# Folding the softmax factor into the masked-maximum pass of a two-layer attention and feed-forward kernel

## The chip, the cores and the metric

The kernel runs on one core of a Trainium2 chip. The metric is the device time of one execution in microseconds (us); lower is better. A profiled execution also has a span, from its first to its last instruction.

## What the kernel must compute

Two pre-norm transformer layers on x of shape (4, 256, 256), all float32. Each layer adds an attention block and then a feed-forward block to x. Only the attentions bear on the change:

```
layer 0:  q = rms_norm(x Wq) ; k = rms_norm(x Wk)          16 query heads, 8 key/value heads, head width 128
          q, k = rope(q), rope(k)
          logits = (q * 0.0884) k^T ;  masked to j <= i and i - j < 128
          probs  = softmax(logits) ;   out = (probs v) Wo
layer 1:  scores = (x Wq)(x Wk)^T                          16 heads, width 128
          masked to j <= i, then / sqrt(128)
          probs  = softmax(...) ;      out = (probs v) Wo
```

The softmax is computed in the stable form: exp of (scaled logit minus the row's largest scaled logit), divided by the row's sum. In layer 0 the query's RMS normalisation is not applied to q: the query's row factor `rms_r` is a factor per row of the logits, so it can be applied after the product q k^T. The feed-forward of layer 0 is a gated one with a 2-of-4 sparsification, that of layer 1 has a Walsh-Hadamard transform that is folded into its second weight matrix.

## The kernel before, in words

Tokens are 1024 rows in 8 tiles of 128. Each attention works on 64 units: 8 head pairs times 4 sequences times 2 heads. A unit is one head of one sequence of 256 rows. Its scores are two blocks, rows 0 to 127 against 128 keys (columns 0 to 127 of a bank) and rows 128 to 255 against 256 keys (columns 128 to 383).

The attention is a software pipeline written out by hand in slots c = -5 to 70. In slot c each engine does a fixed list of pieces, each for another unit or token tile, and semaphores join the engines (`need`, line 62). Slots 11 to 58 are a hardware loop of 3 turns of 16 slots; the slots before and after are written out. The order inside a slot is the program order of each engine:

- TensorE (`pe_slot`, L254): scores of unit c (L250, L251); the projection of piece c+5 (L273 in layer 0, L279 and L308 in layer 1); the output product of piece c-6 (L296); the transposes of unit c-2 (L317); the product with v of unit c-3 (L328, L330); in layer 0 the transposes of tile c+3 (L339).
- ScalarE, ACT (`act_slot`, L345): copies of what TensorE left for units c-3 and c-4 (L352, L360) and of pieces c+4 and c+2 (L368, L370, L377, L384, L392), and last the two exps of unit c (L402). The next slot's copies stand behind these exps in ScalarE's queue.
- VectorE, DVE (`dve_slot`, L460): reciprocal and normalisation of unit c-1 (L411, L414), residual add of piece c-7 (L422), low part of the encoding of unit c-4 (L431), the masked maxima of unit c (L447) and the negated, scaled maxima (L453 in layer 0, L457 in layer 1); in layer 0 then the RMS sums and the rotation of tile c+4 (L482, L486, L490, L493). In the last slots, from 60 on, the maxima come first.
- GpSimd, POOL (`pool_slot`, L504): in layer 0 the power -1/2 that gives `rms_r` and the rest of the rotation (L513, L515, L519); in both layers the splits of the next pair's weights into high and low parts (L500, L502). In slots 1 to 6 of layer 1 it also makes one butterfly of the Hadamard transform per slot (L961).

The masked maximum is one VectorE instruction per block: (scores + mask) * scale, with scale 1, written to `scores`, and the running maximum of it read out to `rowmax`. A small instruction then makes `negmax` = -rowmax * factor, and the exp computes exp(factor * scores + negmax) with the row sum as a second output. The factor is the row factor `rms_r` in layer 0 (an operand of one value per partition) and the constant 1/sqrt(128) in layer 1.

Of the kernel before, what the change touches and what calls it, by code (L numbers as in the profile page):

```python
# [39 lines left out]
RMS_EPS = 1e-6  # L40
ATTN_SCALE = 0.08838834764831845
ROPE_BASE = 10000.0
LOW = -3.0e38
MASKED = -1.0e30
WA = (1024, 1536)
WA_FFN = 2048
# [32 lines left out]
def build(nc, x_in, wa, wax, wb, wdown0, w2t, consts, scales, out):  # L79
    with ExitStack() as ctx:  # L80
        def sb(name, shape, dt=F32):
            return ctx.enter_context(nc.sbuf_tensor(name, shape, dt))

        def sem(name):
# [18 lines left out]
        scores = sb("scores", [P, 2, 384])  # L103
        probs = sb("probs", [P, 4, 384])
        probs_t = sb("probs_t", [P, 2, 384])
        rowmax = sb("rowmax", [P, 2, 2])
        negmax = sb("negmax", [P, 2, 2])
        rowsum = sb("rowsum", [P, 4, 2])
        rinv = sb("rinv", [P, 4, 2])
# [39 lines left out]
        s_scl, s_w2 = sem("scales_loaded"), sem("w2_loaded")  # L149
        s_zero, s_half, s_tab, s_scq = (sem(n) for n in ("zero_set", "half_set", "tables_made", "qscale_made"))  # L150
        ln = {n: sem("ln_" + n) for n in ("stats", "mv", "ve", "r", "xn", "turned", "hi", "lo")}
        names = ("scores", "max", "nb", "exp", "rinv", "pnorm", "pt", "ptev", "pv", "ehi", "elo", "op", "opadd",
                 "proj", "vproj", "qkev", "vev", "sq", "ss", "ms", "rp", "rot", "radd", "roped", "tq", "tqev",
                 "a0hi", "a0", "ahi", "a", "bhi", "b")
        at = [{n: sem(f"L{L}_{n}") for n in names} for L in range(2)]
# [189 lines left out]
        def act_slot(act, L, it, c):  # L345
            s = at[L]

            m = c - 3
            if live(it, m):
                need(act, s["pt"], it, m + 1)  # L350
                need(act, s["pv"], it, m - 1)
                nc.scalar.copy(probs_t[:, m % 2, :], bank[PT_BANK][:, 0:384]).then_inc(s["ptev"], 1)  # L352

            m = c - 4
            if live(it, m):
                u = m % 8
                b, hh = u // 2, u % 2
                need(act, s["pv"], it, m + 1)
                need(act, s["op"], it, m - hh - 6)
                nc.scalar.copy(enc[0][:, hh, b * D:(b + 1) * D], bank[O_BANK][:, 0:D]).then_inc(s["ehi"], 1)  # L360
            m = c + 4
            if live(it, m):
                t = m % 8
                need(act, s["proj"], it, m + 1)
                if L == 0:

                    need(act, s["ss"], it, m)
                    nc.scalar.activation(squares[:, :], bank[PJ_BANK + m % 2][:, 0:384], ACT.Square).then_inc(s["sq"], 1)  # L368
                    need(act, s["pv"], it, m - t % 2 - 14)
                    nc.scalar.copy(v[:, m // 8 % 2, t, 0:DH], bank[PJ_BANK + m % 2][:, 384:512]).then_inc(s["vev"], 1)  # L370
                else:
                    half, w = t // 4, t % 4
                    need(act, s["scores"], it, m - t + 4 * half - 4)
                    if it is None and m in (0, 2):
                        act.wait_ge(ff[0]["lo"], 10 + m)
                        act.wait_ge(ff[0]["lo23"], 2 + m)
                    nc.scalar.copy(qk[:, w, half * 512:(half + 1) * 512], bank[PJ_BANK + m % 2][:, :]).then_inc(s["qkev"], 1)  # L377

                    need(act, s["vproj"], it, m + 1)
                    need(act, s["pv"], it, m - t % 2 - 14)  # L380
                    if it is None and m == 0:

                        act.wait_ge(ff[0]["cmp"], 24)
                    nc.scalar.copy(v[:, m // 8 % 2, t, :], bank[TQ_BANK][:, 0:D]).then_inc(s["vev"], 1)  # L384
            if L == 0:

                m = c + 2
                if live(it, m):
                    t = m % 8
                    need(act, s["tq"], it, m + 1)  # L390
                    need(act, s["scores"], it, m - t % 2 - 6)
                    nc.scalar.copy(qk[:, 0:3, t * P:(t + 1) * P],  # L392
                                   bank[TQ_BANK][:, 0:384].rearrange("p (a t) -> p a t", a=3)).then_inc(s["tqev"], 1)

            if live(it, c):
                u = c % 8
                b, hh = u // 2, u % 2
                need(act, s["nb"], it, c + 1)
                need(act, s["pt"], it, c - 3)
                for r, (c0, c1) in enumerate(((0, 128), (128, 384))):  # L400
                    scale = rms_r[:, 2 * b + r, hh:hh + 1] if L == 0 else float(DH) ** -0.5
                    nc.scalar.activation(probs[:, c % 4, c0:c1], scores[:, c % 2, c0:c1], ACT.Exp,  # L402
                                         bias=negmax[:, c % 2, r:r + 1], scale=scale,
                                         accum_out=rowsum[:, c % 4, r:r + 1]).then_inc(s["exp"], 1)

        def dve_normalise(dve, L, it, c):
# [27 lines left out]
        def dve_scores_wait(dve, L, it, c):  # L434

            s = at[L]
            if live(it, c):
                need(dve, s["scores"], it, c + 1)
                need(dve, s["exp"], it, 2 * c - 2, 2)

        def dve_maxima(dve, L, it, c):

            s = at[L]
            if live(it, c):
                b, hh = c % 8 // 2, c % 2
                for r, (c0, c1) in enumerate(((0, 128), (128, 384))):
                    nc.vector.tensor_tensor_reduce(out=scores[:, c % 2, c0:c1], in0=bank[S_BANK + c % 2][:, c0:c1],  # L447
                                                   in1=mask[L][:, c0:c1], scale=1.0, scalar=LOW, op0=ALU.add, op1=ALU.max,
                                                   accum_out=rowmax[:, c % 2, r:r + 1]).then_inc(s["max"], 1)
                need(dve, s["max"], it, 2 * c + 2, 2)  # L450
                if L == 0:
                    need(dve, s["rp"], it, c - hh + 2)
                    nc.vector.scalar_tensor_tensor(out=negmax[:, c % 2, :], in0=rowmax[:, c % 2, :], scalar=-1.0,  # L453
                                                   in1=rms_r[:, 2 * b:2 * b + 2, hh], op0=ALU.mult,
                                                   op1=ALU.mult).then_inc(s["nb"], 1)
                else:
                    nc.vector.tensor_scalar(negmax[:, c % 2, :], rowmax[:, c % 2, :], -float(DH) ** -0.5, None,  # L457
                                            ALU.mult).then_inc(s["nb"], 1)

        def dve_slot(dve, L, it, c):  # L460
            s = at[L]
# [42 lines left out]
        def pool_slot(pool, L, it, c):  # L504
            s = at[L]
            if L == 0:
                m = c + 3
                if live(it, m):
                    t = m % 8

                    need(pool, s["ms"], it, m + 1)
                    need(pool, s["exp"], it, 2 * (m - t % 2) - 12, 2)
                    nc.gpsimd.tensor_tensor(rms_r[:, t, :], meansq[:, m % 2, :], neg_half[:, 0:3], ALU.pow).then_inc(s["rp"], 1)  # L513
                    need(pool, s["rot"], it, m + 1)
                    nc.gpsimd.tensor_tensor(rot_a[:, m % 2, :], rot_a[:, m % 2, :], rot_b[:, m % 2, :],  # L515
# [590 lines left out]
        def _(dve):  # L1106
# [6 lines left out]
            nc.vector.tensor_tensor(a_w[0][1][:, 0:WA[0]], raw_a[:, 0, 0:WA[0]], a_w[0][0][:, 0:WA[0]].bitcast(F32),  # L1113
                                    ALU.subtract).then_inc(at[0]["a0"], 1)
            dve.wait_ge(s_scl, 16)
            nc.vector.tensor_scalar(scl[:, 0::2, :], scl[:, 0::2, :], ATTN_SCALE, None, ALU.mult).then_inc(s_scq, 1)
            for t in range(4):
                ln_dve_lo(dve, 0, t, 4 + t)

# [90 lines left out]
def shape_constants(np):  # L1210
# [7 lines left out]
    low = np.float32(MASKED)  # L1218
    tri = np.where(past, np.float32(0), low)
    win = np.where(window, np.float32(0), low)  # L1220
    mask0 = np.concatenate([tri, win, tri], 1)
    mask1 = np.concatenate([tri, np.zeros((P, P)), tri], 1)
    frac = np.arange(0, DH, 2, dtype=np.float32) / np.float32(DH)
    timescale = (np.float32(ROPE_BASE) ** frac).astype(np.float32)
# [52 lines left out]
```

## Time and profile before

| what | value |
|---|---|
| time, median of 3 runs | 768.96 us (768.14 to 769.33) |
| span of the profiled execution | 763.1 us |
| median less span (what lies around the span) | 5.9 us |
| PE busy | 712.4 us, 93% of the span |
| DVE busy | 549.9 us, 72% |
| ACT busy | 415.8 us, 54% |
| POOL busy | 404.2 us, 53% |
| mean granted TensorE clock | 0.987 of full |

No time of its own is given for the profiled execution beside its span, so times are compared through the difference to the median. Stages by time from the span's start: start up to about 34 us, attention of layer 0 to about 291 us, feed-forward of layer 0 to about 396 us, attention of layer 1 to about 690 us, feed-forward of layer 1 to the end. The busy time of an engine is that of its instructions; an instruction that is held after it has been handed to its engine counts as busy for as long as it is held.

### The profile page before, as it was taken

The page shows a single profiled execution, that of the slowest core. Times are in us where ns is not written, and L with a number is a line of the kernel's source. Part 1 is how long each engine was busy: PE and PEld are TensorE (multiplying, and loading weights), DVE is VectorE, ACT ScalarE, POOL GpSimd, SP SyncE. Part 2 cuts the span into 40 slices and gives each one's busy share as a digit, 9 for nine tenths or more (in the row PEclk, how much of TensorE's full clock was granted, in tenths as well). Part 3 has the DMA queues.
Part 4 walks back from the last instruction along what each step waited for, and adds up shares of the span by engine and source line. Part 5 has one row for each costly group of instructions (what it writes and reads, how often), then busy time and mean ns, then how long its engine had stood idle before and what let it go on. Part 6 is the DMA issues. An engine that isn't in the chain of part 4 may idle for free.

```text
span 763.1 us, 15137 instructions
## 1 busy us (share of the span) xinstructions
PE 712.4 (93%) x4360; PEld 633.9 (83%) x4360; DVE 549.9 (72%) x1861; ACT 415.8 (54%) x1213; POOL 404.2 (53%) x545
## 2 busy tenths in 40 slices
PE   4899999999999969986888999999999999989998
PEld 3589999899899967775776899999999999877887
DVE  7898987988898897979867655555545555576533
ACT  3577777677677754430344556555555655644221
POOL 4898888788787856526387523233241514416000
PEclk9999999999999999988999999999999999999999
DMA  6011010101110110300101010101010100000000
GB/s 220 2 43 32 12 43 2 42 0 41 58 67 0 55 56 1 110 1 1 42 1 56 1 56 1 56 1 55 0 55 0 60 36 14 1 14 1 1 28 28
DMA packets 9015, 24.75 MB, mean 32 GB/s; under 512 B 896, under 2 KB 3072, under 8 KB 8832
## 3 DMA queue, kind: packets, MB, share of 16 engines
q1 hardware_dynamic: 8240, 22.55, 8.6%
q10 hardware_dynamic: 720, 1.57, 0.6%
q8 instruction: 22, 0.36, 0.2%
q14 instruction: 33, 0.27, 0.1%
HBM read 23.07 MB, written 1.05 MB: 32 GB/s over the span
## 4 chain that ended last, share of the span: by engine, by line
PE 80%; DVE 12%; issue 4%; ACT 1%; POOL 1%; DMA 1%; DVEq 0%; SPq 0%; ACTq 0%; POOLq 0%
PE bank L296 11%; PE bank L597 10%; PE bank L279 10%; PE bank L273 10%; PE bank L328 7%; PE bank L251 6%; PE bank L308 5%; PE bank L317 5%; PE bank L630 5%; PE bank L330 3%; PE bank L250 3%; PE bank L339 3%; DVE work L814 2%; DVE probs L414 1%; PE bank L655 1%
## 5 line engine op out<-in xcount | busy, mean ns | idle before, releaser
L500 POOL TENSOR_TENSOR a_hi<-raw_a,zero 128x384 fp32r<-128x384 f32 (+2 forms) x75 | 60.4, 805 | 116.7 <-PE bank L308 115.0
L431 DVE TENSOR_TENSOR enc_lo<-bank,enc_hi 128x256 fp32r<-128x256 f32 x128 | 54.2, 423 | 74.2 <-PE bank L251 66.0
L402 ACT ACTIVATE probs<-scores,negmax,rms_r 128x128 f32<-128x128 f32 (+1 forms) x128 | 69.1, 540 | 61.1 <-DVE negmax L453 61.1
L414 DVE TENSOR_SCALAR probs<-probs,rinv 128x128 f32<-128x128 f32 (+1 forms) x256 | 90.9, 397 | 4.5
L352 ACT COPY probs_t<-bank 128x384 f32<-128x384 f32 x128 | 60.6, 474 | 57.5 <-PE bank L317 56.6
L402 ACT ACTIVATE probs<-scores,negmax 128x128 f32<-128x128 f32 (+1 forms) x128 | 57.2, 448 | 58.0 <-DVE negmax L457 58.0
L447 DVE CUSTOM_DVE_ANT_0 scores<-bank,cst 128x128 f32<-128x128 f32 (+1 forms) x256 | 80.0, 350 | 3.5 <-PE bank L251 3.5
L296 PE MATMUL bank<-b_hi,enc_hi 128*128 128x256 f32 x256 | 73.7, 288 | 9.3 <-DVE x L422 9.1
L328 PE MATMUL bank<-probs_t,v 128*128 128x256 f32 x256 | 77.0, 383 | 2.9 <-DVE enc_lo L431 2.8
L251 PE MATMUL bank<-qk 128*128 128x256 f32 x256 | 76.9, 382 | 0.0
L502 POOL TENSOR_TENSOR a_lo<-raw_a,a_hi 128x384 fp32r<-128x384 f32 (+2 forms) x75 | 72.8, 970 | 5.9
L513 POOL TENSOR_TENSOR rms_r<-meansq,neg_half 128x3 f32<-128x3 f32 x64 | 57.8, 904 | 33.4 <-DVE meansq L490 33.1
L296 PE MATMUL bank<-b_lo,enc_hi 128*128 128x256 f32 x256 | 72.1, 282 | 0.0
L296 PE MATMUL bank<-b_hi,enc_lo 128*128 128x256 f32 x256 | 72.0, 281 | 0.0
L411 DVE RECIPROCAL rinv<-rowsum 128x2 f32<-128x2 f32 x128 | 20.3, 159 | 66.4 <-ACT probs L402 62.2
L515 POOL TENSOR_TENSOR rot_a<-rot_a,rot_b 128x384 f32<-128x384 f32 x64 | 66.6, 1041 | 0.0
L273 PE MATMUL bank<-a_hi,xT_hi 128*128 128x512 f32 x128 | 62.1, 485 | 4.5 <-DVE rot_b L493 3.5
L279 PE MATMUL bank<-xT_hi,a_hi 128*128 128x512 f32 x128 | 62.1, 485 | 0.9 <-DVE xT_lo L226 0.9
L317 PE MATMUL bank<-cst,probs 128*128 128x128 f32 x384 | 62.7, 272 | 0.2 <-ACT probs_t L352 0.2
L296 PEld LDWEIGHTS bank<-b_hi,enc_hi 128*128 128x128 f32 x256 | 48.3, 189 | 16.8 <-issue 10.4
L360 ACT CAST enc_hi<-bank 128x256 fp32r<-128x256 f32 x128 | 47.6, 372 | 20.7 <-PE bank L330 20.1
L500 POOL TENSOR_TENSOR b_hi<-raw_b,zero 128x128 fp32r<-128x128 f32 (+1 forms) x68 | 30.3, 446 | 47.3 <-PE bank L296 47.3
(106 smaller groups left out, 2216.2 us busy)
## 6 DMA issues: line engine op xcount, KB each, us to landing
raw_a<-in_wa SPq DMA_DIRECT2D x10, 768.0 KB, 4.4
raw_a<-in_wa SPq DMA_DIRECT2D x9, 512.0 KB, 4.4
raw_b<-in_wb SPq DMA_DIRECT2D x16, 256.0 KB, 2.7
x<-in_x SPq DMA_DIRECT2D x4, 256.0 KB, 5.9
w_a<-in_w2t SPq DMA_DIRECT2D x1, 1024.0 KB, 4.8
raw_a<-in_wax SPq DMA_DIRECT2D x2, 512.0 KB, 3.2
raw_b<-in_wdown SPq DMA_DIRECT2D x2, 512.0 KB, 3.8
raw_a<-in_wa ACTq DMA_DIRECT2D x1, 512.0 KB, 4.6
```

Source lines behind the costliest of these rows:

```text
L251: pe.matmul(ps[:, 128:384], qk[:, q, t0 + 128:t0 + 256], qk[:, k, t0:t0 + 256], start=True, stop=True).then_inc(s["scores"], 1)
L273: mm = pe.matmul(ps[:, :], xT[l][:, g, t * P:(t + 1) * P], a_w[slot][r][:, g * 512:(g + 1) * 512], start=i == 0, stop=i == 5)
L279: mm = pe.matmul(ps[:, :], a_w[slot][l][:, g * 768 + w * P:g * 768 + (w + 1) * P], xT[r][:, g, half * 512:(half + 1) * 512], start=i == 0, ...
L296: mm = pe.matmul(output_bank(m)[:, 0:D], enc[l][:, h, t * P:(t + 1) * P], b_w[slot][r][:, h * D:(h + 1) * D], start=i == 0, stop=i == 5)
L317: mm = pe.transpose(bank[PT_BANK][:, j * P:(j + 1) * P], probs[:, m % 4, j * P:(j + 1) * P], ident)
L328: pe.matmul(bank[O_BANK][:, 0:256], v[:, m // 8 % 2, 2 * b, vc:vc + DH], probs_t[:, m % 2, 0:256], start=True, stop=False, skip_group_chec ...
L402: nc.scalar.activation(probs[:, c % 4, c0:c1], scores[:, c % 2, c0:c1], ACT.Exp, bias=negmax[:, c % 2, r:r + 1], scale=scale, accum_out=ro ...
L414: nc.vector.tensor_scalar(probs[:, m % 4, c0:c1], probs[:, m % 4, c0:c1], rinv[:, m % 4, r:r + 1], None, ALU.mult).then_inc(s["pnorm"], 1)
L447: nc.vector.tensor_tensor_reduce(out=scores[:, c % 2, c0:c1], in0=bank[S_BANK + c % 2][:, c0:c1], in1=mask[L][:, c0:c1], scale=1.0, scalar ...
L500: nc.gpsimd.tensor_tensor(hi, src, zero[:, 0:1].broadcast_to(list(src.shape)), ALU.add).then_inc(s_hi, 1)
L502: nc.gpsimd.tensor_tensor(lo, src, hi.bitcast(F32), ALU.subtract).then_inc(s_lo, 1)
L597: mm = pe.matmul(ps[:, :], a_w[t][l][:, c0:c0 + P], xT[rr][:, g, th * 512:(th + 1) * 512], start=q == 0, stop=q == 5)
```

## The change

The factor moves from the exp into the masked-maximum pass. `scale` of the pass becomes the factor, with the sign turned, so what is written to `scores` is minus the scaled logit; the reduction is a minimum instead of a maximum; its result is minus the largest scaled logit, which is `negmax` itself. The instruction that made `negmax` and the tile `rowmax` go away, with the semaphore `nb`. The exp takes `scale=-1.0` in both layers. In layer 1 the factor is the constant -1/sqrt(128). In layer 0 it is the row factor `rms_r`, one value per partition, and the sign comes from the query's scale table and from a mask of the other sign.

The waits move as well: ScalarE waits for each block's own minimum ahead of that block's exp, where it waited once for `nb`; VectorE's wait for `rms_r` stands with the wait for the scores, ahead of L431; GpSimd waits for the minima and not for the exps before it writes `rms_r` again.

```diff
             if live(it, c):
-                u = c % 8
-                b, hh = u // 2, u % 2
-                need(act, s["nb"], it, c + 1)
                 need(act, s["pt"], it, c - 3)
                 for r, (c0, c1) in enumerate(((0, 128), (128, 384))):
-                    scale = rms_r[:, 2 * b + r, hh:hh + 1] if L == 0 else float(DH) ** -0.5
+                    need(act, s["max"], it, 2 * c + 1 + r, 2)
                     nc.scalar.activation(probs[:, c % 4, c0:c1], scores[:, c % 2, c0:c1], ACT.Exp,
-                                         bias=negmax[:, c % 2, r:r + 1], scale=scale,
+                                         bias=negmax[:, c % 2, r:r + 1], scale=-1.0,
                                          accum_out=rowsum[:, c % 4, r:r + 1]).then_inc(s["exp"], 1)
...
                 need(dve, s["scores"], it, c + 1)
                 need(dve, s["exp"], it, 2 * c - 2, 2)
+                if L == 0:
+                    need(dve, s["rp"], it, c - c % 2 + 2)
...
                 for r, (c0, c1) in enumerate(((0, 128), (128, 384))):
+                    scale = rms_r[:, 2 * b + r, hh:hh + 1] if L == 0 else -float(DH) ** -0.5
                     nc.vector.tensor_tensor_reduce(out=scores[:, c % 2, c0:c1], in0=bank[S_BANK + c % 2][:, c0:c1],
-                                                   in1=mask[L][:, c0:c1], scale=1.0, scalar=LOW, op0=ALU.add, op1=ALU.max,
-                                                   accum_out=rowmax[:, c % 2, r:r + 1]).then_inc(s["max"], 1)
-                need(dve, s["max"], it, 2 * c + 2, 2)
-                if L == 0:
-                    need(dve, s["rp"], it, c - hh + 2)
-                    nc.vector.scalar_tensor_tensor(out=negmax[:, c % 2, :], in0=rowmax[:, c % 2, :], scalar=-1.0,
-                                                   in1=rms_r[:, 2 * b:2 * b + 2, hh], op0=ALU.mult,
-                                                   op1=ALU.mult).then_inc(s["nb"], 1)
-                else:
-                    nc.vector.tensor_scalar(negmax[:, c % 2, :], rowmax[:, c % 2, :], -float(DH) ** -0.5, None,
-                                            ALU.mult).then_inc(s["nb"], 1)
+                                                   in1=mask[L][:, c0:c1], scale=scale, scalar=HIGH, op0=ALU.add, op1=ALU.min,
+                                                   accum_out=negmax[:, c % 2, r:r + 1]).then_inc(s["max"], 1)
...
-                    need(pool, s["exp"], it, 2 * (m - t % 2) - 12, 2)
+                    need(pool, s["max"], it, 2 * (m - t % 2) - 12, 2)
                     nc.gpsimd.tensor_tensor(rms_r[:, t, :], meansq[:, m % 2, :], neg_half[:, 0:3], ALU.pow).then_inc(s["rp"], 1)
...
-            nc.vector.tensor_scalar(scl[:, 0::2, :], scl[:, 0::2, :], ATTN_SCALE, None, ALU.mult).then_inc(s_scq, 1)
+            nc.vector.tensor_scalar(scl[:, 0::2, :], scl[:, 0::2, :], -ATTN_SCALE, None, ALU.mult).then_inc(s_scq, 1)
...
-    mask0 = np.concatenate([tri, win, tri], 1)
+    mask0 = -np.concatenate([tri, win, tri], 1)
```

## Rows read from the trace of the kernel before

**Rows 1.** The profile page: busy time of each engine, and the chain that ended last.

```profile
PE 712.4 (93%) x4360; PEld 633.9 (83%) x4360; DVE 549.9 (72%) x1861; ACT 415.8 (54%) x1213; POOL 404.2 (53%) x545
...
PE 80%; DVE 12%; issue 4%; ACT 1%; POOL 1%; DMA 1%; DVEq 0%; SPq 0%; ACTq 0%; POOLq 0%
```

**Rows 2.** Busy time by window: stretch, length, busy (instructions), clock, DMA share, GB/s.

```profile
50.00:127.90 77.90, 77.90 (x503) 71.26 (x502) 70.06 (x271) 56.71 (x176) 65.11 (x98) 1.00 0.07 22
...
262.00:291.00 29.00, 22.30 (x157) 19.64 (x156) 26.60 (x92) 15.67 (x48) 17.15 (x21) 1.00 0.12 37
...
400.00:426.00 26.00, 20.91 (x110) 16.94 (x108) 20.39 (x41) 10.87 (x36) 21.40 (x19) 0.93 0.11 41
426.00:670.00 244.00, 241.83 (x1578) 222.31 (x1579) 132.84 (x563) 142.88 (x443) 78.73 (x113) 1.00 0.08 26
670.00:694.00 24.00, 21.43 (x129) 17.14 (x128) 17.02 (x69) 10.92 (x33) 3.91 (x7) 1.00 0.05 12
```

**Rows 3.** Groups of instructions by form, whole span: busy us, mean ns, idle before.

```profile
L447 DVE CUSTOM_DVE_ANT_0 scores<-bank,cst 128x256 f32<-128x256 f32 x128 | 53.6, 419 | 0.0
...
L402 ACT ACTIVATE probs<-scores,negmax,rms_r 128x256 f32<-128x256 f32 x64 | 37.5, 586 | 0.0
...
L402 ACT ACTIVATE probs<-scores,negmax 128x256 f32<-128x256 f32 x64 | 31.6, 494 | 0.0
...
L457 DVE TENSOR_SCALAR negmax<-rowmax 128x2 f32<-128x2 f32 x64 | 18.1, 283 | 2.2
L453 DVE SCALAR_TENSOR_TENSOR negmax<-rowmax,rms_r 128x2 f32<-128x2 f32 x64 | 16.3, 255 | 2.2
```

**Rows 4.** VectorE groups by form in 670 to 691 us, GpSimd nearly idle.

```profile
L206 DVE TENSOR_SCALAR xn<-x,ln_mv,ln_r 128x256 f32<-128x256 f32 x4 | 1.6, 398 | 0.0
...
L414 DVE TENSOR_SCALAR probs<-probs,rinv 128x256 f32<-128x256 f32 x3 | 1.0, 348 | 0.0
```

**Rows 5.** TensorE's waits, 396 to 428 us: total us, times, longest.

```profile
PE bank L308 <- ACT v L384: 3.5, 4, 1.3
PE bank L328 <- DVE enc_lo L431: 1.7, 2, 0.8
```

**Rows 6.** Timeline of VectorE in layer 1's first slots: start, duration (us).

```profile
400.22 2.17 DVE L457 TENSOR_SCALAR negmax<-rowmax 128x2 f32<-128x2 f32 x1
...
406.52 0.17 DVE L457 TENSOR_SCALAR negmax<-rowmax 128x2 f32<-128x2 f32 x1
...
411.73 0.28 DVE L447 CUSTOM_DVE_ANT_0 scores<-bank,cst 128x128 f32<-128x128 f32 x1
...
415.32 2.88 DVE L414 TENSOR_SCALAR probs<-probs,rinv 128x128 f32<-128x128 f32 x2
...
419.11 2.34 DVE L457 TENSOR_SCALAR negmax<-rowmax 128x2 f32<-128x2 f32 x1
```

**Rows 7.** Timeline of GpSimd in the same slots.

```profile
399.98 2.38 POOL L961 TENSOR_TENSOR work<-w_a 128x1024 f32<-128x1024 f32 x1
...
411.62 2.42 POOL L961 TENSOR_TENSOR w_a<-work 128x1024 f32<-128x1024 f32 x1
...
419.08 2.35 POOL L961 TENSOR_TENSOR work<-w_a 128x1024 f32<-128x1024 f32 x1
```

**Rows 8.** Timeline of TensorE: the same matmuls in two slots.

```profile
412.79 0.60 PE L328 MATMUL bank<-probs_t,v 128*128 128x256 f32 x2
...
415.26 0.40 PE L279 MATMUL bank<-xT_hi,a_lo 128*128 128x512 f32 x1
...
418.67 0.87 PE L328 MATMUL bank<-probs_t,v 128*128 128x256 f32 x2 [0.83 <-DVE enc_lo L431]
...
422.85 0.40 PE L279 MATMUL bank<-xT_hi,a_lo 128*128 128x512 f32 x1
```

**Rows 9.** The end of layer 0's attention, 262 to 284 us: VectorE group, TensorE's wait.

```profile
L453 DVE SCALAR_TENSOR_TENSOR negmax<-rowmax,rms_r 128x2 f32<-128x2 f32 x5 | 2.8, 558 | 0.2
```

```profile
PE bank L296 <- DVE x L422: 5.0, 3, 3.0
```

More of the change, by code:

```diff
@@ L42 @@
 ROPE_BASE = 10000.0
-LOW = -3.0e38
+HIGH = 3.0e38
 MASKED = -1.0e30
@@ L105, in build @@
         probs_t = sb("probs_t", [P, 2, 384])
-        rowmax = sb("rowmax", [P, 2, 2])
         negmax = sb("negmax", [P, 2, 2])
@@ L151, in build @@
         ln = {n: sem("ln_" + n) for n in ("stats", "mv", "ve", "r", "xn", "turned", "hi", "lo")}
-        names = ("scores", "max", "nb", "exp", "rinv", "pnorm", "pt", "ptev", "pv", "ehi", "elo", "op", "opadd",
+        names = ("scores", "max", "exp", "rinv", "pnorm", "pt", "ptev", "pv", "ehi", "elo", "op", "opadd",
                  "proj", "vproj", "qkev", "vev", "sq", "ss", "ms", "rp", "rot", "radd", "roped", "tq", "tqev",
```

## The prediction, made before the changed kernel ran

> **What bounds the kernel now.** I read the page first, then the windows by stage, the waits of TensorE, and the timelines of the stretches in which TensorE stands still. The page says that TensorE is busy 93% of the span and makes up 80% of the chain that ended last, VectorE 12% [rows 1]. So a VectorE instruction less is worth nothing on average; the question is where TensorE waits for VectorE. The windows answer it [rows 2]. In the steady slots of layer 0 (50 to 127.9 us) TensorE is busy 77.90 of 77.90 us, in those of layer 1 (426 to 670 us) 241.83 of 244. TensorE stands still at the end of layer 0's attention (6.7 of 29.0 us), in the first slots of layer 1's attention (5.1 of 26.0 us, with the granted clock down to 0.93) and at that attention's end (2.6 of 24.0 us). Only these stretches can pay.
>
> The first slots of layer 1 carry my forecast. The small instruction L457 has 64 instances with a mean of 283 ns [rows 3], but it is not the same everywhere: 0.17 us at 406.52, and 2.17 us at 400.22 and 2.34 us at 419.11 [rows 6]. The GpSimd rows explain these two: the Hadamard butterflies L961 run from 399.98 to 402.36 and from 419.08 to 421.43, and L457 ends at 402.39 and 421.45, just behind them [rows 7]. It is held while GpSimd works. L414 is held too (2.88 us for two at 415.32), while L447 is not: at 411.73 it takes its usual 0.28 us in the midst of the butterfly that began at 411.62 [rows 6, 7]. Behind a held L457 stands the exp, behind the exp the next slot's copies of ScalarE, and TensorE waits for the copy L384 four times, 3.5 us, and for L431 twice, 1.7 us [rows 5].
>
> **The change part by part.** *Layer 1, first slots.* L457 goes, with 5 instances between 399 and 426 us. Undisturbed it is 0.17 us; the two that I show cost 2.0 and 2.2 us more. A third such case has the same pattern behind the butterfly of 411.62. What is late next is L414, which needs a gap between GpSimd instructions for each of its two halves. Before, a slot took three such gaps (L457, L414, L414) and an exp between them, so that slots locked to two butterflies each: the held L457 at 419.11 follows a held L414 at 415.32. After, one slot needs two gaps, and from the second of them to the next L414 lie L431, half of L447, two exps of one block each, and L411, roughly 1.9 us; so a slot locks to one butterfly, and these come on average 3.7 us apart (411.62 and 419.08 are two butterflies apart [rows 7]). TensorE's own slot there is about as long. Walking the queues of the four engines through slots 0 to 6 with these durations, the copies and the enc_lo are ready 1 to 5 us before TensorE gets to them, and all six waits close. That is 3.5 + 1.7 = 5.2 us [rows 5]. The exp of the first block may also start before the second block's minimum, 0.42 us earlier by L447's mean [rows 3]; that only adds to the margin.
>
> The waits also carry a lower clock. In one slot the matmuls from the first L328 to the last L279 take from 412.79 to 415.66, 2.87 us; in the next from 418.67 to 423.25, 4.58 us, though nothing among them waits [rows 8]. Just before, TensorE had waited, the last time for 0.83 us [rows 8]; part of the second run is at the lower of its two levels (1.2 against 2.4 GHz). With the waits gone I take the 1.7 us as gone too. Bounds: 5.2 + 1.7 = 6.9 us if all closes; 2.0 us if L414 takes over what L457 leaves. I take 6.9, since the hand-made walk leaves margin at each of the six.
>
> *Layer 0, last slots.* TensorE waits 5.0 us in three places for the residual add L422 [rows 9], which stands in VectorE's queue behind L447, L453, L411 and L414. Five L453 there take 558 ns in the mean, 2.8 us in all [rows 9]; with 0.17 us each for the work, as L457 takes when nothing holds it [rows 6], 1.9 us of it is holding. It does not all come back: L414 is next in the queue and meets the same GpSimd instructions. In my walk the first slot gives nothing (L414's second half ends behind the same GpSimd instruction), the second 0.3 us, the third about 1 us. Bounds: 0 (L414 takes all) to 2.8 us; I take 1.2, nearer to the walk.
>
> *Layer 0, the added operand.* The pass now reads one value per partition. No row before has that on a reduction with a PSUM input. Nearest: L206 with two such operands takes 398 ns at 128x256, L414 with one takes 348 [rows 4], so about 50 ns for one. Two passes make 0.10 us a slot, against L453's mean of 0.26 us that goes [rows 3]. Bounds per pass: 0, to 92 ns, which is what the row factor costs the exp (586 against 494 ns [rows 3]). In the steady slots all of it lies beside TensorE: 503 matmuls at 26 a slot are 19.3 slots of 4.03 us, in which VectorE idles 7.84 us, 0.41 us a slot [rows 2]. So even 2 x 92 ns with no saving at all costs nothing. The cover is gone at 0.41 us a slot.
>
> *The exps.* In layer 0 they lose 92 ns each and start earlier; in layer 1 their scale was a constant already. ScalarE is busy 56.7 of 77.9 us [rows 2], so this is hidden except in the last slots, where it is within the 1.2.
>
> *The moved waits.* VectorE's wait for `rms_r` now stands ahead of L431 and L447. In slot c it asks for tile c+1 at most, which GpSimd made two slots earlier, so it is met. GpSimd's wait for minima in place of exps is for a unit four slots back, met either way. No DMA moves. The sign changes in the tables cost nothing: same instructions.
>
> *The rest.* In the start, VectorE's queue is on the chain for a few slots, and so it is for one instruction's worth at each turn of the loop in layer 0: 0.3 us in all (0 to 0.8). At the end of layer 1's attention TensorE is idle 2.6 us, most of it behind the layer norm and the held L414; 0.2 us (0 to 1). In the steady slots of layer 1 nothing.
>
> **Sum.** 6.9 + 1.2 + 0.3 + 0.2 = 8.6 us. The span 763.1 becomes 754.5; the median lies 5.9 us above the span before, and so the time is 768.96 - 8.6 = 760.4 us. All of it is carried to the end, because what follows each stretch hangs on TensorE or on the work right behind it.
>
> **The rivals.** *A. The lock moves on.* L414 takes the holding that L457 leaves in layer 1: only the 2.0 us of the first L457, and half of layer 0's 1.2, come back. For it: L414 is held already, 2.88 us at 415.32. Against it: a slot needs one GpSimd gap less. 768.96 - 2.6 - 0.5 = 765.9 us.
>
> *B. The waits close but the clock does not stay up*, since TensorE has other short waits just before this stretch and merely loses the clock elsewhere: 1.7 us less, 762.1 us.
>
> *C. The new pass is held by GpSimd in layer 0.* Slower than before. With its row factor in SBUF the pass has two SBUF operands, as L453 has, and each of the two passes of a slot then waits for a gap. GpSimd is busy 65.1 of 77.9 us with 98 instructions, 0.66 us each [rows 2]; the first pass waits 0.84 x 0.66 / 2 = 0.3 us, the second for the whole next instruction, 0.66 us. With 0.10 for the operand that is 1.06 us, less 0.26 for L453: 0.8 us a slot against a cover of 0.41. Slots get 0.39 us longer in about 58 steady slots, 22.6 us: 768.96 + 22.6 - 6.9 = 784.7 us. It decides from 0.41 us a slot on. Against it: L453 itself, with two SBUF operands, is held only 0.1 us in the mean, and by the same mean the two passes would add 0.04 us net and stay covered.
>
> The Trainium skill (SBUF — State Buffer, Who interferes with whom) speaks against the change here: VectorE and GpSimd share one pair of ports, locked for a whole instruction, and a VectorE instruction contends for it in a 2-port mode or with two SBUF inputs, but not with at most one. It does not say whether a value per partition counts as an input. If it does, case C is the result and the time 784.7 us; if not, the forecast stands. The trace agrees with the rule for L447, one SBUF input and not held inside a butterfly [rows 6, 7]; no row before shows a pass with the added value.
>
> *D. No change*, because TensorE is busy 93% of the time and the waits in layer 1's first slots have another cause such as the first exp's table load: 768.9 us. Against it: waits of VectorE and ScalarE that end with the butterflies.
>
> **How the numbers follow.** The forecast has 0.66, A 0.11, B 0.12, C 0.05 (with other ways to be slower 0.07), D 0.04. A measurement of this kernel tells 0.2%, 1.5 us, from no change. Faster: 0.66 + 0.11 + 0.12 = 0.89; same 0.04; slower 0.07. The range reaches down to 757.0 us (layer 0's end at its 2.8 in place of 1.2, the start and layer 1's end at 1.8 in place of 0.5: 757.5, and a little for closer packing) and up to 765.0 us (half-way from B to A and beyond), which leaves out C, D and most of A, under 0.2.
>
> **What would show it.** Right: no instruction between L447's second half and L411 or L482; TensorE's waits for L384 and L431 in layer 1's first slots gone, and granted clock 1.00 in that window, its slots 3.7 us each; the longest L414 still 2 to 3 us; the pass in layer 0 at about 470 ns for 128x256 (419 + 50), in layer 1 still 419; exps of layer 0 at 494 ns; the steady slot of layer 0 still 4.03 us. Wrong: a pass in layer 0 with a mean over 0.7 us and a longer slot (C); TensorE still waiting for L384 behind an exp that is late because L414 was held (A); a lower clock somewhere else in attention 1 (B); slots 0 to 5 of layer 1 as long as before (D).

## The result, and the profile after

| | median | range | ratio to before, 95% interval |
|---|---|---|---|
| before | 768.55 us (4 runs) | 767.78 to 769.33 | |
| changed | 758.55 us (4 runs) | 754.81 to 759.08 | 0.9863 (0.9837 to 0.9889) |

The forecast was 760.4 us, range 757.0 to 765.0. The medians lie 10.0 us apart (8.5 to 12.5 by the interval of the ratio); I had said 8.6.

The page after gives the engines' busy times and the chain, which answer to [rows 1]. TensorE's share of the chain rises from 80 to 86%, VectorE's falls from 12 to 8%.

```profile
PE 713.8 (94%) x4360; PEld 637.9 (84%) x4360; DVE 519.8 (69%) x1733; ACT 409.6 (54%) x1213; POOL 404.5 (53%) x545
...
PE 86%; DVE 8%; issue 3%; POOL 1%; DMA 1%; ACT 1%; SPq 0%; DVEq 0%; ACTq 0%; POOLq 0%
```

Now the stretches of [rows 2] in the changed kernel (same columns: stretch, length, TensorE, its loads, VectorE, ScalarE, GpSimd, clock, DMA share, GB/s). The steady slots of layer 0 are TensorE's as before. In the first slots of layer 1 TensorE is busy 24.08 of 25.00 us at clock 1.00, where it was busy 20.91 of 26.00 us at 0.93. But the end of layer 0's attention shows a clock of 0.86 and that of layer 1 one of 0.94, which the first profile had at 1.00.

```profile
50.00:127.90 77.90, 77.90 (x502) 71.16 (x501) 67.61 (x252) 53.55 (x174) 64.98 (x98) 1.00 0.07 22
...
260.00:285.00 25.00, 21.23 (x132) 19.27 (x131) 19.77 (x69) 12.78 (x42) 15.91 (x18) 0.86 0.14 50
...
395.00:420.00 25.00, 24.08 (x143) 21.33 (x144) 16.59 (x52) 17.08 (x50) 22.70 (x23) 1.00 0.12 43
...
660.00:690.00 30.00, 26.57 (x149) 21.69 (x150) 20.22 (x80) 11.98 (x35) 6.60 (x11) 0.94 0.04 10
```

The groups by form answer to [rows 3]. The pass with a value per partition takes 479 ns for 128x256, with a constant 419; the exps are of one kind. L453 and L457 are gone. (Line numbers shift: the pass L447 is L446 now, the exp L402 is L398, the normalisation L414 is L410, the residual add L422 is L418, the product L296 is L295.)

```profile
L398 ACT ACTIVATE probs<-scores,negmax 128x256 f32<-128x256 f32 x128 | 64.1, 501 | 0.0
...
L446 DVE CUSTOM_DVE_ANT_0 scores<-bank,cst,rms_r 128x256 f32<-128x256 f32 x64 | 30.7, 479 | 0.0
L446 DVE CUSTOM_DVE_ANT_0 scores<-bank,cst 128x256 f32<-128x256 f32 x64 | 26.8, 419 | 0.0
```

The shortest, median and longest of all 128 passes with a value per partition, of both widths (ns, then first and last start):

```profile
L446 DVE CUSTOM_DVE_ANT_0 scores<-bank,cst,rms_r x128: 332/410/483, 27.5 to 277.7; 128x128 f32<-128x128 f32 x64, 128x256 f32<-128x256 f32 x64
```

TensorE's waits from 392 to 425 us, the answer to [rows 5]: those for the copy L384 and for L431 are gone, and what is left, the layer norm ahead of the first slot, was there before (0.9 and 0.2 us as well).

```profile
PE bank L278 <- DVE xT_lo L225: 0.9, 1, 0.9
PE bank L212 <- DVE xn L205: 0.2, 1, 0.2
```

VectorE and GpSimd in three of these slots (two timelines; start, duration): L410, the normalisation, is still held, 1.8 to 2.3 us for its two halves, but nothing else is, and each of these slots has one butterfly (L951, which was L961). VectorE's passes start at 408.22, 412.29, 415.95 and 419.73, so 3.7 to 4.1 us apart.

```profile
408.22 0.28 DVE L446 CUSTOM_DVE_ANT_0 scores<-bank,cst 128x128 f32<-128x128 f32 x1
...
409.77 2.26 DVE L410 TENSOR_SCALAR probs<-probs,rinv 128x128 f32<-128x128 f32 x2
...
412.29 0.28 DVE L446 CUSTOM_DVE_ANT_0 scores<-bank,cst 128x128 f32<-128x128 f32 x1
...
413.89 1.80 DVE L410 TENSOR_SCALAR probs<-probs,rinv 128x128 f32<-128x128 f32 x2
...
415.95 0.28 DVE L446 CUSTOM_DVE_ANT_0 scores<-bank,cst 128x128 f32<-128x128 f32 x1
...
419.73 0.27 DVE L446 CUSTOM_DVE_ANT_0 scores<-bank,cst 128x128 f32<-128x128 f32 x1
```

```profile
409.15 2.37 POOL L951 TENSOR_TENSOR w_a<-work 128x1024 f32<-128x1024 f32 x1
...
412.38 2.38 POOL L951 TENSOR_TENSOR w_a<-work 128x1024 f32<-128x1024 f32 x1
```

**Where the time went, by stage.** The stages are cut at the first matmul of the feed-forward of layer 0, at the first and at the last projection of layer 1's attention. "Clock" is TensorE's busy time times (1 - granted clock), summed over windows of 2 us, for the four stages in order. It is an estimate of the most that the lower clock can have cost: where TensorE would otherwise have waited, slower matmuls cost nothing.

| profile | span | layer 0 attention | feed-forward 0 | layer 1 attention | rest | of it clock |
|---|---|---|---|---|---|---|
| before, first | 763.1 | 292.0 | 85.6 | 281.8 | 103.7 | 0 + 7.9 + 1.5 + 0 |
| before, second | 767.4 | 294.4 | 84.7 | 284.7 | 103.6 | 4.4 + 5.3 + 3.1 + 0 |
| changed, first | 757.1 | 291.1 | 86.5 | 274.3 | 105.2 | 3.0 + 7.6 + 0 + 1.7 |
| changed, second | 751.1 | 289.6 | 83.4 | 274.5 | 103.6 | 0 + 5.3 + 0 + 0 |

Layer 1's attention is 7.3 to 10.4 us shorter. Layer 0's is 0.9 to 4.8 us shorter, and that depends on which executions one compares. The rest differs by its clock share. The feed-forward of layer 0 does not: without that share it has 77.7, 79.4, 78.9 and 78.1 us. Part of this is only where the cut before it falls, so layer 0 is better read as both its stages together without their clock shares: 369.7 and 369.4 us before, 367.0 and 367.7 after, 1.7 to 2.7 us shorter. The spans also say how far one pair of profiles can mislead: the two first ones lie 6.0 us apart, the two second ones 16.3.

### The profile page after: what moved, and what is told of

Its sections match the earlier page's. It is cut to its first block, busy times and chain, and to the rows that moved or that the text cites. A ratio compares the mean times of both kernels' runs of the same rounds, so it can differ in the third digit from the quotient of the medians.

```text
span 757.1 us, 15084 instructions
## 1 busy us (share of the span) xinstructions
PE 713.8 (94%) x4360; PEld 637.9 (84%) x4360; DVE 519.8 (69%) x1733; ACT 409.6 (54%) x1213; POOL 404.5 (53%) x545
## 4 chain that ended last, share of the span: by engine, by line
PE 86%; DVE 8%; issue 3%; POOL 1%; DMA 1%; ACT 1%; SPq 0%; DVEq 0%; ACTq 0%; POOLq 0%
PE bank L295 12%; PE bank L278 11%; PE bank L272 10%; PE bank L587 10%; PE bank L327 7%; PE bank L250 7%; PE bank L307 6%; PE bank L316 5%; PE bank L620 5%; PE bank L329 4%; PE bank L249 4%; PE bank L338 3%; DVE work L804 2%; PE bank L645 1%; DMA x<-in_x 1%
## 5 line engine op out<-in xcount | busy, mean ns | idle before, releaser
L398 ACT ACTIVATE probs<-scores,negmax 128x128 f32<-128x128 f32 (+1 forms) x256 | 115.5, 452 | 42.5 <-DVE negmax L446 41.9
L427 DVE TENSOR_TENSOR enc_lo<-bank,enc_hi 128x256 fp32r<-128x256 f32 x128 | 54.2, 424 | 121.7 <-PE bank L250 111.0
L410 DVE TENSOR_SCALAR probs<-probs,rinv 128x128 f32<-128x128 f32 (+1 forms) x256 | 86.7, 380 | 4.5
L295 PE MATMUL bank<-b_hi,enc_hi 128*128 128x256 f32 x256 | 75.4, 294 | 5.9 <-DVE x L418 5.9
L295 PE MATMUL bank<-b_hi,enc_lo 128*128 128x256 f32 x256 | 72.7, 284 | 0.0
L295 PE MATMUL bank<-b_lo,enc_hi 128*128 128x256 f32 x256 | 72.7, 284 | 0.0
L295 PEld LDWEIGHTS bank<-b_hi,enc_hi 128*128 128x128 f32 x256 | 49.0, 191 | 11.6 <-issue 7.3
L329 PEld LDWEIGHTS bank<-probs_t,v 128*128 128x128 f32 x256 | 49.3, 193 | 6.9
L688 ACT ACTIVATE gate<-bank 128x512 f32<-128x512 f32 x32 | 19.0, 598 | 64.6 <-PE bank L587 56.2
L418 DVE TENSOR_TENSOR x<-bank,x 128x256 f32<-128x256 f32 x128 | 53.2, 416 | 0.0
```

The costliest lines, as they stand in the source:

```text
L295: mm = pe.matmul(output_bank(m)[:, 0:D], enc[l][:, h, t * P:(t + 1) * P], b_w[slot][r][:, h * D:(h + 1) * D], start=i == 0, stop=i == 5)
L329: pe.matmul(bank[O_BANK][:, 128:256], v[:, m // 8 % 2, 2 * b + 1, vc:vc + DH], probs_t[:, m % 2, 256:384], start=False, stop=True, skip_gr ...
L410: nc.vector.tensor_scalar(probs[:, m % 4, c0:c1], probs[:, m % 4, c0:c1], rinv[:, m % 4, r:r + 1], None, ALU.mult).then_inc(s["pnorm"], 1)
```

## The experiments

All kernels are compared with the kernel before on the same chip. Ratios have their 95% interval. A gain in us below is worked out from the ratio unless two medians are named.

**Layer 1 alone** (`l1_only`) and **layer 0 alone** (`l0_only`). The edit is the change itself with `if L == 1` or `if L == 0` around it, the other layer as before (the kernel is abridged here):

```diff
+                if L == 1:
+                    ... tensor_tensor_reduce(..., scale=-float(DH) ** -0.5, op1=ALU.min, accum_out=negmax[...])
+                else:
                     ... as before, with rowmax and L453
```

> The change in layer 1 alone; layer 0 as before. Theory (the small instruction L457 was held by GpSimd's butterflies in layer 1's first slots): nearly all of the gain of the whole change, 9 to 10 us of the 10.0, so a ratio of 0.988 to 0.991; TensorE's waits for L384 and L431 in the first slots gone. Rival (the gain is a bit less VectorE work in every place, in both layers alike): about half of it, ratio 0.994.

> The change in layer 0 alone; layer 1 as before. Theory: 0 to 2 us faster (0.9975 to 1.000), the steady slot still 4.03 us, all of it at the end of layer 0's attention; the waits in layer 1's first slots (5.2 us) still there. Rival (both layers alike): 5 us faster, ratio 0.994. If the operand of one value per partition were held by GpSimd, the pass would take over 700 ns for 128x256 here.

Measured: layer 1 alone 759.04 us, ratio 0.9895 (0.9873 to 0.9917), so 8 us; layer 0 alone 764.32 us, 0.996 (0.994 to 0.9979), so 3 us. Multiplied, the two ratios make 0.9855. The theory expected 9 to 10 us (a ratio of 0.988 to 0.991) and 0 to 2 us; the rival 5 and 5. Most is layer 1's, but layer 0 is worth more than either the theory's share or my forecast of 1.5. TensorE's waits in layer 1's first slots with layer 0 changed alone are those of before, to the tenth:

```profile
PE bank L309 <- ACT v L385: 3.5, 4, 1.3
PE bank L329 <- DVE enc_lo L437: 1.7, 2, 0.8
```

and with layer 1 changed alone only the layer norm's are left. With layer 0 changed alone the pass with a value per partition takes 479 ns as well.

**The small instruction in its place, but not held** (`l1_unheld`). The kernel before, one instruction exchanged for a form that was never held in the profile (L411). The kernel leaves out the factor: the exp of layer 1 subtracts another number than the scaled maximum, in the same time.

```diff
-                    nc.vector.tensor_scalar(negmax[:, c % 2, :], rowmax[:, c % 2, :], -float(DH) ** -0.5, None,
-                                            ALU.mult).then_inc(s["nb"], 1)
+                    nc.vector.reciprocal(negmax[:, c % 2, :], rowmax[:, c % 2, :]).then_inc(s["nb"], 1)
```

> The kernel before, but layer 1's L457 is a reciprocal of the same two columns: the same place, the same waits, about the same 0.16 us, in a form that is never held (L411). The factor's value is not computed, so layer 1's softmax is not the reference's. Theory (the lock): nearly the whole gain of the change in layer 1 comes back although no instruction is removed: 6 to 9 us faster, ratio 0.988 to 0.992. Rival (an instruction less in the chain and the exp's earlier start make the gain): within 1.5 us of the kernel before.

Measured: 760.71 us, ratio 0.9912 (0.989 to 0.9933), 6.8 us faster than before with not one instruction less. In its trace L457 is a reciprocal of 166 ns mean (283 before) and 167 ns at most, also where it starts in the midst of a butterfly, as at 413.36 us beside the one from 412.79 to 415.18; and TensorE waits for neither copy nor enc_lo in the first slots. This is the run that settles the cause: it is the holding. What is left for the rival, an instruction less in the chain, is the difference of this kernel to layer 1 alone, 1.3 us by the ratios, and their intervals overlap, so it is not told from nothing.

```profile
L457 DVE RECIPROCAL negmax<-rowmax 128x2 f32<-128x2 f32 x64 | 10.6, 166 | 2.2
```

```profile
413.36 0.17 DVE L457 RECIPROCAL negmax<-rowmax 128x2 f32<-128x2 f32 x1
```

**Short butterflies** (`small_bf_before`, `small_bf_after`). The other side of the holding: GpSimd's L961 is cut to 8 columns, in the kernel before and in the changed one. Both leave out nearly all of the Hadamard transform. The cut takes away what holds L457 and what holds the normalisation alike.

```diff
-                nc.gpsimd.tensor_tensor(b[:, :, n % 2, :], a[:, :, 0, :], a[:, :, 1, :],
+                nc.gpsimd.tensor_tensor(b[:, 0:1, n % 2, 0:8], a[:, 0:1, 0, 0:8], a[:, 0:1, 1, 0:8],
```

> The kernel before with the six Hadamard butterflies on GpSimd cut to 8 columns (the transform of the weights is left out but for these, so layer 1's feed-forward is not the reference's). Theory (the long GpSimd instructions hold L457): L457's mean falls from 283 ns to under 200, TensorE's waits in layer 1's first slots close, 6 to 9 us faster than the kernel before with the small instruction still in place, ratio 0.988 to 0.992. Rival (the instruction's own place in the chain costs): under 2 us faster.

> The changed kernel with the same small butterflies. Theory: without the long instructions the change is worth only what it is worth in layer 0 and a little in layer 1's last slots: 2 to 4 us faster than the kernel before with small butterflies, and within 1.5 us of the changed kernel, ratio to the kernel before 0.985 to 0.988. Rival: the full 10 us again, so 8 us or more between the two kernels with small butterflies.

Measured: before with short butterflies 759.97 us, ratio 0.9893 (0.9868 to 0.9917); the same with the change 756.89 us, 0.9847 (0.9813 to 0.9881). So the short butterflies alone give 8 us with L457 left as it is, and the change on top of them 3 us by the medians, as much as layer 0 alone gives. L457's mean fell only to 203 ns, not under 200: the weight splits hold it as well, for shorter (0.36 us at 402.92, behind the split from 402.86 to 403.26). The group:

```profile
L457 DVE TENSOR_SCALAR negmax<-rowmax 128x2 f32<-128x2 f32 x64 | 13.0, 203 | 2.2
```

**One wait for both minima** (`both_minima`). The changed kernel, with the exp's earlier start taken away:

```diff
-                    need(act, s["max"], it, 2 * c + 1 + r, 2)
+                    need(act, s["max"], it, 2 * c + 2, 2)
```

> The changed kernel, but both exps of a unit wait for both minima, as before, in place of each for its own. Theory: the earlier start only adds margin; time within 0.2% of the changed kernel (758.6 us), at most 1 us later. Rival (the exp's earlier start is a main part of the gain): 3 us or more slower than the changed kernel, 762 us or later.

Measured: 756.84 us, ratio 0.9854 (0.9825 to 0.9882), not to be told from the changed kernel. The earlier start is worth nothing that these runs can show.

**The two kernels again** (`after_again`, `before_again`).

> The changed kernel once more, unedited, as the yardstick of this set. Both theories: ratio 0.9863 as before, within its interval 0.984 to 0.989; executions spread over some 4 us with the mean granted clock (0.982 to 0.99).

> The kernel before, unedited, for a second profile. Its executions range from 764.8 to 771.5 us with the granted clock, and the profile I predicted from has the span of the fastest of them. Theory: the stretches without a lower clock are as long as in the first profile within 0.5 us, and whatever the span has above 763 us is clock, in stages where TensorE waits. Rival: another wait that the first profile did not have.

Measured: the changed kernel 757.92 us (753.02 to 760.58, more than the 4 us of spread I expected), ratio 0.9874 (0.9843 to 0.9904). The second profile of before, with a time of 769.03 us and a span of 767.4, is in the table above. Its clock fell at the end of layer 0's attention and longer than before in layer 1's first slots, after 424 us. But the rival is partly right too: the stretches without a lower clock are not as long within 0.5 us. TensorE waits 5.2 us for the copy L384 (3.5 in the first profile), in longer single waits (2.3 against 1.3 us). VectorE's side is the same in both: its passes L447 for slots 0 to 6 lie between 399.54 and 429.71 us in the first profile, 30.2 us, and between 401.06 and 431.25 in the second, 30.2 us too. What differs is TensorE's clock. In the first profile it was low around 421 us (0.50 from 420 to 422), TensorE came later to its next wait, and that wait was 0.67 us; in the second the clock was still full there and the same wait was 2.34 us. So the low clock of the first profile cost nothing on top of the waits. In the second it fell behind the last held slot and did cost: TensorE's slot from 429.03 us took 6.47 us, where the first profile has 4.46. At the end of layer 0 TensorE waits 3.9 us for L422 against 5.0; there too the clock is the lower one in the second profile (0.50 in the windows from 270 to 278 us).

The same wait in the first profile and in the second, then the second profile's sums and windows:

```profile
423.92 0.39 PE L308 MATMUL bank<-a_hi,xT_hi 128*128 128x256 f32 x1 [0.67 <-ACT v L384]
```

```profile
425.48 0.39 PE L308 MATMUL bank<-a_hi,xT_hi 128*128 128x256 f32 x1 [2.34 <-ACT v L384]
```

```profile
PE bank L308 <- ACT v L384: 5.2, 4, 2.3
PE bank L328 <- DVE enc_lo L431: 1.6, 2, 0.8
```

```profile
424.00:428.00 4.00, 1.79 (x10) 1.48 (x11) 3.90 (x8) 1.43 (x5) 3.92 (x3) 0.82 0.00 0
428.00:432.00 4.00, 4.00 (x12) 3.28 (x12) 2.84 (x12) 2.38 (x8) 3.56 (x7) 0.50 0.01 2
```

**The turns of layer 0's loop** (`padded`, `padded_one`). In the kernel before VectorE stood still for 2.07 and 2.14 us at the two turns of layer 0's loop, with no releaser ("issue"), and TensorE then waited 0.6 us for L422. In every kernel with layer 0 changed both are gone; in all in which layer 0 is as before they are there. Its loop body had shrunk from 271 to 254 instructions, counted without those that only wait for a semaphore, and the traffic of one instruction queue over the whole execution from 33 packets to 22. This is the stall in the first profile of before, and the queue before and after:

```profile
130.51 0.55 DVE L493 TENSOR_TENSOR rot_b<-bank,sin_t 128x384 f32<-128x384 f32 x1
133.13 0.17 DVE L411 RECIPROCAL rinv<-rowsum 128x2 f32<-128x2 f32 x1 [2.07 <-issue]
```

```profile
q14 instruction: 33, 0.27, 0.1%
```

```profile
q14 instruction: 22, 0.18, 0.1%
```

The edits to the changed kernel, 17 short instructions in the loop body or one long one:

```diff
+                    for i in range((1 + (c == LOOP_FROM)) if it is not None else 0):
+                        nc.vector.memset(scratch[:, 2 * (c - LOOP_FROM) + i:2 * (c - LOOP_FROM) + i + 1], 0.0)
```
```diff
+                    if it is not None and c == LOOP_FROM + LOOP_STEP - 1:
+                        nc.vector.memset(scratch[:, :], 0.0)
```

> The changed kernel with 17 one-column memsets of an unused tile added to VectorE's loop body of layer 0, one per slot and two in the first, so that the body has as many instructions as before (271; the changed kernel has 254). In the kernel before VectorE stood still for 2.1 us at each of the two turns of this loop with no releaser, and TensorE then waited 0.6 us for the residual add; in the changed kernel neither is there. Theory (the length of the body decides whether a turn stalls): the two stalls of 2.1 us are back, TensorE waits 0.2 to 0.6 us at each turn, layer 0's attention 0.5 to 1.2 us longer. Rival (the shorter VectorE work gives slack enough to hide the turn): no stall, as the memsets take about 0.07 us a slot of 0.5 us of slack.

> Control to the padded kernel: one memset of 512 columns in the last slot of layer 0's VectorE loop body, so more work right before the turn but 255 instructions. Theory of the length: no stall at the turns. Rival (slack): a stall or a wait of TensorE at the turns as in the padded kernel.

Measured: no stall in either, 758.68 us, ratio 0.9888 (0.9849 to 0.9926), and 759.51 us in one execution. In the padded kernel VectorE goes over the turn from 131.29 to 131.76, and TensorE is busy 212.00 of 212.00 us from 50 to 262 (210.82 in the kernel before). So 271 instructions without the waits do not bring the stall back. But the padding did not restore the whole body: with the instructions that only wait for a semaphore counted, it has 332 before, 313 in the changed kernel and 317 in the padded one, since 13 memsets carry a wait that had been an instruction of its own. The length of the body is therefore not ruled out.

```profile
131.29 0.55 DVE L486 TENSOR_TENSOR rot_b<-bank,sin_t 128x384 f32<-128x384 f32 x1
131.76 0.15 DVE L408 RECIPROCAL rinv<-rowsum 128x2 f32<-128x2 f32 x1
```

Slack isn't the cause: before, VectorE itself stood still for 2.07 us with nothing to wait for, and more slack would hide such a stall, not remove it. What the stall goes with is the loading of instructions. In the five profiles that have it (both of before, layer 1 alone, the unheld instruction, before with short butterflies) the instruction queue q14 brings three packets of 8 KB around each turn, between 127 and 137 us and between 192 and 205 us (at 129.0, 131.2 and 133.9 us in the first profile, whose stall is from 131.06 to 133.13), and 33 in all; in the nine without it q14 brings none from 120 to 260 us, and 22 or 23 in all, the padded kernel among them. So the body is loaded again at each turn only where VectorE stalls. That it stalls because it waits for these packets is the reading at hand, not shown by an edit. What decides whether the body is loaded again, its whole length or where it lies in the stream (it begins behind 262 instructions before, 249 in the changed and the padded kernels, waits counted), was not tried and stays open.

**The residual add first** (`residual_first`, `residual_both`). After the change TensorE still waits 3.1 us for L418 at the end of layer 0's attention and 2.8 us at that of layer 1, because the residual add stands behind a held normalisation that it does not need. The edit swaps two lines in the slots from 60 on; the second kernel has the single wait of `both_minima` as well.

```diff
                 dve_maxima(dve, L, it, c)
-                dve_normalise(dve, L, it, c)
                 dve_residual(dve, L, it, c)
+                dve_normalise(dve, L, it, c)
```

> The changed kernel with the residual add ahead of the normalisation on VectorE in the last slots (from 60 on) of both layers. TensorE waits there for the residual add (3.1 us in layer 0, 2.8 us in layer 1 in the profile after), which stands behind a held L410. Theory (the hold is what is left): these waits shrink by half or more, 2 to 4 us faster than the changed kernel, ratio 0.981 to 0.984. Rival (the next piece, the transposes, needs the normalised rows anyway): within 1 us of it.

> The changed kernel with the residual add ahead of the normalisation in the last slots, and both exps waiting for both minima. Theory: the exp's wait is worth nothing either way, so the same time as with the residual add ahead alone, ratio 0.979 within 0.003. Rival (the single wait is cheaper on ScalarE's sequencer, by which the kernel with it looked a little faster): 1 to 2 us faster still, ratio 0.977.

Measured: 751.76 us (750.57 to 752.36), ratio 0.9791 (0.9765 to 0.9817), more than the theory's 0.981 to 0.984, and 751.58 us (749.17 to 752.34), 0.9784 (0.9756 to 0.9812). Both beat the kernel before and the changed one: 6 to 7 us faster than the latter's medians. The wait for L418 at the end of layer 0 falls to 1.4 us, at the end of layer 1 to 0.7 us:

```profile
PE bank L295 <- DVE x L418: 1.4, 2, 1.2
```

That is 3.8 us less waiting for L418 (5.9 to 2.1), of which 0.6 us comes back as longer waits for enc_lo, L427 (1.2 to 1.8). Not all of it is time: against the second profile of the changed kernel, which like both of these shows no lower clock in either attention, the spans are 2.5 and 2.0 us shorter (751.1 against 748.6 and 749.1). The rest of the 6 to 7 us would then be clock that does not fall in the usual execution. For it: the executions of the two kernels lie within 1.8 and 3.2 us of each other, where those of the changed kernel lie within 7.6. How often the clock would fall in other executions is not shown.

## Why the prediction was right, point by point

- *TensorE is the bound, and only where it waits can the change pay*: right. The steady slot of layer 0 has the same length, and VectorE's 30.1 us less of busy time (549.9 to 519.8) brought 10.0.
- *L457 held by the butterflies, six waits of TensorE behind it*: right, and shown three ways: another form of the instruction, shorter butterflies, and the change in layer 1 alone each close the waits and give 7 to 8 us.
- *Layer 1's first slots, 6.9 us, of it 1.7 clock*: a little small. Layer 1 alone gives 8 us by the runs, and its attention is 7.3 us shorter than in the profile I read. From the scores of this attention's first unit to those of its ninth TensorE took 37.0 us in that profile and takes 28.7 after, 8.3 less; the steady slots behind them went from 4.45 to 4.47 us, where I had put no change, and take 1 us of it back. The 1.7 us was not a loss of its own: the second profile has it as waiting. The sum of waits and slow matmuls was the right one to take all the same. That profile was a lucky one. The profiled span was 763.1, and spans of 763.2 to 763.6 belong to times of 764.8 to 765.2 us; the median execution of before has a span of some 766.5. In the second profile this attention took 10.2 to 10.4 us more than after the change.
- *What lies around the span*, 5.9 us: wrong. I took the median for the profiled execution's time. In the runs of before it is 1.6 us, in those of after 1.9 to 2.0; the other 4.3 us of the difference are the lower clock and longer waits of the usual execution. I priced from the best execution and left out that the waits which go also carry most of its spread in layer 1.
- *Layer 0, 1.2 us at its end and 0.3 elsewhere*: the mis-sized term, 3 us (1.6 to 4.6 by the interval) by the run of layer 0 alone. In its profile the waits for L422 at the end fall from 5.0 to 4.0 us, close to my 1.2. The turns of the loop bring 1.2 us (TensorE idle 1.18 us from 50 to 262 before, 0 after), where I had put one instruction's worth of queue; I had seen the stalls and not asked whether they would stay. The waits of TensorE for rot_b in the start fall from 3.5 to 3.1 us. That the whole came out 1.4 us from the forecast is partly luck: the 1.2 us of the turns have a cause that the prediction does not know, and the two first profiles differ by 6.0 us, not 8.6.
- *The end of layer 1's attention, 0.2 us*: about right, within the uncertainty. The waits for L422 there are 2.9 us before and 2.8 after, the others the same, and in the first profile after the clock fell there as well.
- *A value per partition costs 50 ns, and a pass is not held by GpSimd*: right; 60 ns measured (479 against 419), and the longest pass of all 128 took 483 ns. Rival C is out: an operand of one value per partition did not make the pass wait, though GpSimd is busy 65 of 78 us beside it.
- *The exps lose 92 ns in layer 0*: about right: 507 ns in layer 0 against 586, so 79. *Their earlier start only adds margin*: right, worth nothing that the runs show.
- *Moved waits cost nothing*: right as far as the profile shows; neither VectorE nor ScalarE waits for `rms_r` in it.
- Rival A (the lock moves on to L414) did not happen in time: L410 is held, up to 2.3 us for its two halves, and TensorE does not wait for it in the first slots. Rival B (the clock falls elsewhere) happened in part: in the first profile after, the clock fell at the ends of both attentions, 4.7 us there by the estimate above. But at the end of layer 0's attention it does so in the second profile of before too (4.4 us), so that part need not be the change's doing. Rival D is out.

## What to carry to other kernels

Look at a small instruction's longest durations and not at its mean: one that reads and writes two columns can be busy 2 us, and the timeline of the other engine then names what holds it. Such a hold can be removed by the form of the instruction as well as by removing the instruction, and what that is worth is decided by which queue stands behind it. Put an instruction that another engine waits for ahead of one that can be held; and before pricing from a profile, place its span among the spans of the timed runs.

## What the runs showed of the hardware

- A float32 VectorE instruction from SBUF to SBUF in `tensor_scalar` form was held until the GpSimd instruction beside it ended: 2.34 us behind a butterfly of 2.35 us, where it takes 0.17 us undisturbed. A reciprocal of the same two columns, also from SBUF, was not: 166 ns in the mean and 167 at most beside the same butterflies. Nor was a reduction pass with PSUM, SBUF and a value per partition: 483 ns at most.
- TensorE's clock is part of what a wait costs, but only where TensorE is the bound. Before, layer 1's attention has 1.5 or 3.1 us of lower clock after runs of waits, and the 1.5 cost nothing beyond the waits; in the eleven profiles of kernels in which the waits are closed its first slots have none. Six executions of the changed kernel spread by 7.6 us, the slower the lower their mean clock (0.991 at 753.0 us, 0.980 at 760.6).
- A stall of 2.07 us of VectorE at the turn of a hardware loop went away with an edit in and ahead of the body. It is there in the five profiles in which packets of an instruction queue arrive at each turn, and absent in the nine in which none do.
